# A transformer block in ten Blocks: POOL's drain left out at five of the Block ends

## The reference

```
x = x + attention(layernorm(x))     # 16 heads of 8, causal softmax, plus a linear "memory" product on e = v[1:] - y[:-1]
x = x + ffn(layernorm(x))           # a shared expert + the best 2 of 8 experts, weighted by gates
x = x + mamba(layernorm(x))         # conv, softplus steps, scan over 1024 positions of 256 x 16 states
x = x + ffn(layernorm(x))
```

## Time and profile before

| | |
|---|---|
| median of 3 runs | 1902.08 us (1888.44 to 1910.78) |
| the profiled execution | 1923.11 us, of which the span of the program's instructions is 1921.4 us |
| projections, from the start | 0 to 90 us |
| attention | 90 to 619 us |
| memory stage | 619 to 744 us |
| ffn1: routing, experts | 744 to 881 to 1032 us |
| state scan | 1032 to 1604 us |
| ffn2: routing, experts | 1604 to 1746 to 1897.6 us |
| join and `clear_all` | 1897.6 to 1921.4 us |

### The profile page before, as it was taken

How to read it: one execution, slowest core, us unless ns; L and a number is a source line. 1 busy time by engine, 2 the same in 40 slices (tenths; PEclk the granted TensorE clock), 3 DMA queues, 4 the chain that set the end, 5 groups by cost and what they waited for, 6 DMA issues and landing times. The chain is left out here.

```text
span 1921.4 us, 27825 instructions
## 1 busy us (share of the span) xinstructions
PE 1397.9 (73%) x8207; PEld 699.9 (36%) x8208; DVE 1270.6 (66%) x2979; ACT 847.5 (44%) x1215; POOL 879.2 (46%) x773
## 2 busy tenths in 40 slices
PE   3459999999999996666884786675875454556883
PEld 1113333333332564445773221221321112435772
DVE  4667999998993566533332388999989995523333
ACT  3404666666667341112442677485573321112441
POOL 3401121121123553652554158879687664652552
PEclk9657999999999897787997797787886666877997
DMA  4721111111121325212223476958859635214225
GB/s 133 232 81 40 49 60 42 56 54 43 61 67 36 87 79 154 65 63 81 78 77 102 141 187 174 235 156 213 200 137 237 153 110 153 64 57 126 76 75 153
DMA packets 218312, 210.68 MB, mean 110 GB/s; under 512 B 49247, under 2 KB 188482, under 8 KB 215874
## 3 DMA queue, kind: packets, MB, share of 16 engines
q1 hardware_dynamic: 196174, 180.70, 35.0%
q0 software_dynamic: 9216, 19.02, 3.0%
q10 hardware_dynamic: 12800, 9.46, 1.6%
HBM read 145.27 MB, written 63.37 MB: 109 GB/s over the span
## 5 line engine op out<-in xcount | busy, mean ns | idle before, releaser
L804 ACT ACTIVATE attn_prob<-attn_ps_cols 128x1024 f32<-128x1024 f32 (+1 forms) x320 | 292.0, 940 | 219.6 <-PE attn_ps_cols L680 218.6
L2386 POOL TENSOR_TENSOR ssm_hc<-ssm_h,ssm_cb 128x1024 f32<-128x1024 f32 x128 | 300.8, 2357 | 137.3 <-DVE ssm_h L2369 113.5
L2369 DVE TENSOR_TENSOR_SCAN ssm_h<-ssm_decay,ssm_ps_u 128x1024 f32<-128x1024 f32 x128 | 292.7, 2287 | 30.9 <-ACT ssm_decay L2357 15.2
L830 POOL TENSOR_SCALAR_AFFINE_SELECT attn_prob<-attn_prob 128x512 f32<-128x512 f32 x128 | 81.2, 634 | 415.9 <-ACT attn_prob L804 415.9
L712 DVE CUSTOM_DVE_ANT_0 attn_ps_rows<-attn_ps_rows,const_mask_rows 128x384 f32<-128x384 f32 (+3 forms) x512 | 236.1, 523 | 39.5 <-PE attn_ps_rows L647 37.4
L647 PE MATMUL attn_ps_rows<-attn_ks,attn_qs 72*128 72x512 bf16 (+3 forms) x768 | 228.9, 352 | 44.2 <-DMA attn_qs<-parts_dram 30.9
L2357 ACT ACTIVATE ssm_decay<-ssm_wide,ssm_aneg 128x1024 f32<-128x1024 f32 x128 | 146.0, 1146 | 173.3 <-DVE ssm_h L2369 97.1
L2320 PE MATMUL ssm_ps_u<-ssm_stack,ssm_spread 96*128 96x512 bf16 x256 | 97.3, 471 | 154.3 <-DVE ssm_h L2369 148.1
L680 PE MATMUL attn_ps_cols<-attn_qs,attn_ks 75*128 75x512 bf16 (+3 forms) x768 | 194.4, 334 | 4.6 <-DMA attn_qs<-attn_nrows 3.9
L699 PE MATMUL attn_ps_o<-attn_prob,attn_vw 128*32 128x512 f32 (+3 forms) x1536 | 166.6, 507 | 0.3 <-POOL attn_prob L830 0.3
L717 DVE TENSOR_REDUCE attn_nm<-attn_ps_rows 128x1 f32<-128x512 f32 x256 | 157.8, 682 | 7.8 <-PE attn_ps_rows L647 7.7
(11 more groups left out here) (340 smaller groups left out, 2515.4 us busy)
## 6 DMA issues: line engine op xcount, KB each, us to landing
ssm_wide<-delta_dram SPq DMA_DIRECT2D x128, 512.0 KB, 6.3
attn_ks<-parts_dram SPq DMA_DIRECT2D x48, 192.0 KB
attn_qs<-parts_dram SPq DMA_DIRECT2D x48, 192.0 KB
parts_dram<-proj_parts SPq DMA_DIRECT2D x8, 768.0 KB, 3.8
ffn1e_x<-ex_dram SPq DMA_DIRECT2D x40, 130.0 KB
ffn2e_x<-ex_dram SPq DMA_DIRECT2D x40, 130.0 KB
split_dram<-ssm_parts SPq DMA_DIRECT2D x6, 768.0 KB, 4.4
ssm_stack<-split_dram SPq DMA_DIRECT2D x18, 256.0 KB, 4.6
```

What stands on the lines that cost most here:

```text
L804: nc.scalar.activation(prob[u % RING][:, heads[0]:heads[-1] + 1, 0:w], ps_cols[s % 2][:].rearrange("p b (x q) -> p (b x) q", x=len(heads) ...
L2369: nc.vector.tensor_tensor_scan(h[t % H_RING][:], decay[t % DECAY_RING][:], ps_u[t % 2][:], 0.0, ALU.mult, ALU.add).then_inc(scan_done, 1)
L2386: nc.gpsimd.tensor_tensor(hc[:, t % HC_RING, :], h[t % H_RING][:], cb[b % 2][:], ALU.mult).then_inc(hc_done, 1)
```

## The change

Five of the Blocks get `no_gpsimd_drain=True`: projections, attention, memory stage, join and state scan. The Blocks of the constants and of `clear_all` stay as they are.

```diff
@@ project @@
-        with nc.Block() as block:
+        with nc.Block(no_gpsimd_drain=True) as block:
```

## The result

The changed kernel took 1926.48 us (median of 5, 1922.42 to 1932.60) beside 1905.97 us of the kernel before (median of 5, 1888.44 to 1921.00): a ratio of 1.0105, 95% interval 1.0073 to 1.0138. Slower, and by more than the forecast half per cent. Three of those five executions of the kernel before are the three that were known when the prediction was made; the two new ones took 1905.97 and 1921.00 us. Three later comparisons of the same two kernels, with 12 executions of the changed one each, gave 1.0047 (1.0028 to 1.0066), 1.0055 (1.0032 to 1.0079) and 1.0036 (1.0009 to 1.0063). The medians lie 9.3, 8.3 and 8.7 us apart in them; the ratios are not those of the medians, and taken times the time of before they make 8.5, 9.9 and 6.9 us. So the size to explain is some 9 us; the first number's other 11 us come up again at the end.

The account below looks back on a forecast made before the run. No single engine was taken to bound the kernel, a row of Blocks at whose ends all five engines meet. 0 + 9.17 + 0.25 = +9.4 us on 1902.1 gave 1911.5 us, range 1898 to 1924.

Parts of the forecast that it names:

- The five DRAINs give back nothing: At the five edited Block ends, POOL's DRAIN ends before the last engine arrives, so removing it gives back 0 us.
- The work moves to line 69 and is exposed there: At the last Block, POOL's DRAIN takes over work previously hidden by the join's transfers; 9.2 us, with nothing hiding it.
- Term one: At line 69, the last Block, POOL's DRAIN grows from 0.046 to 9.216 us, adding 9.17 us.
- The short DRAINs: At the constants' end and line 69, POOL DRAINs with no software DMA before them took 0.041 and 0.046 us.
- What it scales with: At line 69, either one price per DRAIN, 9.2 us, or 0.064 us per software DMA, 18.4 us for 288.
- a fixed price per DRAIN that finds the software queue used: At line 69, the first POOL DRAIN after software DMAs costs 9.2 us whatever their number; the choice taken, chance 0.65.
- the rival: At line 69, the DRAIN costs 0.064 us per software DMA, 18.4 us for 288; 1920.7 us in all, chance 0.2.
- The added barrier steps, 0 to 0.5 us for five: At the five edited ends, four engines count in by a separate instruction; 0.05 us each, +0.25 us in all.
- What lies around the span: Outside the profiled span, time stays the same: span 1921.4 of 1923.1 us before, 1930.8 of 1932.5 after.
- The software queue without its reset: In ffn2, software DMAs run with no POOL DRAIN since ffn1; 0 to +3 us, taken as 0.
- the range's term for scatter: For the whole kernel's time, each case carries a median's scatter, put at 7 us from three runs 22 us apart.
- the scaling case: At line 69, the DRAIN's price grows with software DMAs to 18.4 us; 1920.7 us in all, chance 0.2.

## Why the prediction was wrong, point by point

**The five DRAINs give back nothing:** right. With all five gone and that of line 69 too the ratio is 0.9998 (0.9979 to 1.0017), with four gone and the join's kept 0.9991 (0.9975 to 1.0007). Each had ended before the last engine came, by 2.9 to 13 us (the scan's cover is 3.0 and not 2.9: 1604.5 - 1601.5), and removing what no one waits for changed no end. No stage got shorter by clearly more than the profiles of one kernel differ: the scan took 570 us in place of 573, and 566 us in the last profile of the kernel before.

**The work moves to line 69 and is exposed there:** right, in place and in size. Term one was 9.216 - 0.046 = +9.17 us; the row shows 9.218, so +9.17 us, SP's wait there grew from 1.0 to 10.2 us as put down, and leaving out that last DRAIN brings back all of the loss (0.9998).

**The short DRAINs.** The prediction had a POOL DRAIN with no software DMA before it pay next to nothing. It does: with nothing left to do it takes 34 to 53 ns in these runs.

**What it scales with:** the forecast's side of the alternative held here, 9.2 us and not 18.4, but "a fixed price per DRAIN that finds the software queue used" is wrong as a rule. The price is 0.082 us for each DMA up to 112, then 9.2 us. The two rows of before stood both above the ceiling, where the price no longer depends on the count, and 9.216 = 144 x 0.064 was a coincidence that the rival rested on. So the right 9.2 us came from a wrong rule, by the luck that all counts here, 144 and 288, are above 112; the prediction had called it a leaning and no proof. With fewer DMAs than 112 the answer would have been other.

**The added barrier steps, 0 to 0.5 us for five:** the rows of the five ends add up to some 0.2 us, two of them 0.1 us longer and three the same, against +0.25; four ends together are below what the comparison sees (0.9991, 0.9975 to 1.0007).

**What lies around the span** was put at no change. It is 2.0 to 2.2 us in every execution of the changed kernel and 1.7 to 1.8 us in every later one of the kernel before, so the sum lacked 0.3 to 0.4 us, for which no run gives the reason.

**The software queue without its reset:** ffn2's DMAs at 962 and 963 ns against 960 and 963; nothing. All that the runs show of a "reset" is that a DRAIN's price counts only the DMAs since the last one, as the 7.891 us for the 96 of ffn2's 144 behind the DRAIN inside its routing show.

**The step that failed is the range's term for scatter,** "the scatter of a median, which I put at 7 us". The mechanism held, and its terms came out at +9.17 and some +0.2 us for a sum of +9.4. The range left 12.5 us above the forecast of 1911.5, sized by the scaling case with hardly any room for scatter on top of the likeliest one. Measured was 1926.48, 15.0 us above. Of these, 3.9 us are the median of before, which two more executions moved from 1902.1 to 1905.97; 11.1 us are what the difference of the medians, +20.5 us, has over +9.4.

What the runs show in its place: four comparisons gave 1.0105, 1.0047, 1.0055 and 1.0036. The three with 12 executions of the changed kernel agree with one another and with the 9.2 us of the row; the first, with 5 and 5, lies outside all three of their intervals, though its own interval just touches one of them (1.0073 and 1.0079). Its excess of 11 us is not in the profiled pair: less line 69, the changed kernel's profiled execution was 4.9 us shorter than that of before (1925.7 - 9.2 = 1916.5 against 1921.4). It isn't a property of slow chips, since the fourth comparison ran on one and gave the least.

Part of the excess lies in which executions of before were counted. The profiled one, 1923.11 us, isn't among its five, while the changed kernel's is; with it the median is 1908.4 and the difference 18.1 us. Against the two executions that were new, mean 1913.5 us, the difference is 13.0 us. The lowest is one of the three from before the prediction, 1888.44 us, where the 35 later executions of this kernel on the slow chip of the fourth comparison (23 and 12) don't get below 1899.37.

That the rest is scatter of a small sample is argued and not shown. It would have to be a rare draw: by an estimate from the fourth comparison's executions, five drawn at random of the 12 of the changed kernel and five of the 35 of before give medians 20.5 us or more apart about once in eighty times, and a median of five scatters by 4 us there, less than the 7 us of the prediction. The excess did not come back in three comparisons, and no run tells what made the early executions fast, so its cause stays open.

## What to carry to other kernels

In these runs a drain that ended ahead of the barrier's last comer cost nothing, and taking it out gained nothing (0.9991 with four of them out); before taking it out ask what it settles that a later drain will then have to, and whether anything covers that one. Here POOL's drain behind indirect DMAs had up to 9.2 us of its own work, the join's transfers hid it, and the last Block had nothing to hide it with. So either keep one POOL drain in a stage in which POOL is idle (0.9991), or leave out every one from there to the end (0.9998, in a kernel in which POOL itself waits for the landing of all its DMAs); a drain left out in the middle with one kept at the end was the case that cost (1.0036 to 1.0055 in the four later comparisons, the join's edit alone among them).

## What the runs showed of the hardware that I had not expected

- A POOL DRAIN takes 0.03 to 0.05 us where POOL has issued no DMA since the last and has no work left, and 0.082 us for each indirect DMA otherwise, up to 9.2 us at 112 and flat to 288. At line 69 of the changed kernel it did so with all landed and no packet moving in 1916.3 to 1925.4. The measured counts are those of the table.
- Hiding places differ by chip. The kernel before took 1906 and 1914 us in two jobs and 1804 and 1802 us in two others, on two other chips. The difference lies in the two mixtures of experts: routing and experts of ffn1 took 287 us in the first profile and 234 in that of the join's edit alone, on a fast chip, the state scan 573 and 570. POOL's idle time before the 80 indirect DMAs of ffn2's experts is 92.3 us in the earlier trace rows and 50.9 us in the changed kernel on a fast chip, the DMAs themselves the same:

```profile
L1861 POOL DMA_INDIRECT ey_dram<-ffn2e_out,ffn2e_x x80 | 76.6, 957 | 50.9 <-ACT ffn2e_out L1835 38.3 <-issue 12.3 <-DMA ey_dram<-ffn2e_out,ffn2e_x 0.3
```

  On the two fast chips POOL came last at the routing's end in all six profiles without DRAINs inside the routing, 3.0 to 7.2 us behind SP's DRAIN, with its own drain (846.1 behind 839.8) or without (848.8 behind 842.7); in the kernel before, in the first profile, SP did, by 10.5 and 17.2 us. So a cover that was read on one chip was gone on another. What makes the chips differ, no run shows.
- The time around the span is 2.0 to 2.2 us in the kernels with all five edits, 1.7 to 1.8 us in the kernel before and with the join's edit alone, and 1.8 to 1.9 us with the four others.
